# Second stage of a two-stage attention and mixture-of-experts block: bias rows as a matrix product, row sums from the residual addition, squared differences on ScalarE, fewer router steps, a new VectorE order

## The reference

```python
h = layernorm(x) * (1 + ca) + sa
x = x + ga * linear_attention(h)          # ends in out @ w_proj.T + b_proj
h = layernorm(x) * (1 + cb) + sb
x = x + gb * ffn(h)
# ffn: router_input = h * rsqrt(mean(h*h) + 1e-6) * 512**-0.5 * router_scale
#      logits = router_input @ router_logits            (8 experts)
#      probs = softmax(logits); two largest are chosen
#      weights = probs / sum(probs of the chosen two)
#      out = sum over the two of weight * per_expert_scale * expert(h)
```

## Time and profile before

| | |
|---|---|
| median of 3 runs | 2304.57 us (2302.24 to 2309.63) |
| the profiled execution | 2285.14 us, its span 2283.4 us |
| busy: PE, DVE, ACT, POOL | 91%, 62%, 33%, 39% of the span |
| second stage, about | 613 us to 1086 us after the span's start |
| DVE, PE, POOL busy from 699.6 to 1031.6 us | 299.6, 268.7, 252.0 us of 332 |
| granted TensorE clock there | 0.89 |

### The profile page before, as it was taken

One profiled execution on the slowest core, in us unless ns is written; L12 is line 12 of the kernel. 1 busy time (PEld: TensorE's weight loads), 2 busy tenths in 40 slices (PEclk: granted clock), 3 DMA queues, 4 the chain that ended last, 5 costly groups with the idle time before them and its releaser, 6 DMA issues.

```text
span 2283.4 us, 42310 instructions
## 1 busy us (share of the span) xinstructions
PE 2088.3 (91%) x9344; PEld 1632.4 (71%) x9345; DVE 1420.9 (62%) x3309; ACT 757.3 (33%) x1363; POOL 890.2 (39%) x689
## 2 busy tenths in 40 slices
PE   7999999999987888874899999999999989999997
PEld 5688878888655555553678887887778768778886
DVE  6555655565379999895366665665556556556664
ACT  4244434344334344432133332332223223223332
POOL 4475656667427777775011111111111111111111
PEclk9999999999988899986899999999999999999998
DMA  7576555565625566557755557557675775765554
GB/s 244 190 245 206 170 198 162 199 210 189 216 74 187 201 221 227 192 181 289 216 133 129 130 130 222 131 131 195 157 209 130 212 228 131 188 165 128 130 115 79
DMA packets 293177, 404.88 MB, mean 177 GB/s; under 512 B 50510, under 2 KB 188750, under 8 KB 285262
## 3 DMA queue, kind: packets, MB, share of 16 engines
q1 hardware_dynamic: 165104, 257.57, 35.5%
q0 software_dynamic: 30640, 74.29, 15.6%
q10 hardware_dynamic: 97200, 70.82, 9.8%
HBM read 210.57 MB, written 191.98 MB: 176 GB/s over the span
## 4 chain that ended last, share of the span: by engine, by line
PE 42%; DMA 6%; DVE 1%; issue 1%; ACTq 1%; ACT 0%; DVEq 0%; POOL 0%; SPq 0%
PE bank L1774 42%; DMA arow<-act_rows 3%; DMA act_rows<-hact 3%; ACTq L1031 1%; DVE hact L1663 0%; DVE x_t_lo L1657 0%; DVE gbr L1699 0%; DVE act_t_lo L1674 0%; ACT gact L1020 0%; DVEq L1681 0%; DMA meta<-expert_rows 0%; DMA expert_rows<-rows,dest 0%; SPq L551 0%; ACT x_t_hi L1015 0%; DVE orow L1702 0%
## 5 line engine op out<-in xcount | busy, mean ns | idle before, releaser
L1774 PE MATMUL bank<-wbuf,x_t_hi 128*128 x2160 | 679.5, 396 | 46.5 <-DVE x_t_lo L1657 46.1
L782 POOL DMA_INDIRECT out_rows<-orow,cur_tok x135 | 209.0, 1548 | 985.4 <-DVE orow L1702 917.0
L1774 PEld LDWEIGHTS bank<-wbuf,x_t_hi 128*128 128x128 f32 x2160 | 409.4, 190 | 141.1 <-issue 50.7
L1774 PE MATMUL bank<-wbuf,x_t_lo 128*128 x1080 | 424.6, 393 | 0.0
L1774 PE MATMUL bank<-wbuf,act_t_hi 128*128 x1080 | 346.3, 403 | 30.1 <-DVE act_t_lo L1674 29.7
L1663 DVE TENSOR_TENSOR hact<-bank,gact 128x512 f32<-128x512 f32 x135 | 93.2, 691 | 336.9 <-PE bank L1774 301.0
L1774 PEld LDWEIGHTS bank<-wbuf,act_t_hi 128*128 128x128 f32 x1080 | 208.1, 193 | 80.3 <-issue 34.4
L1774 PEld LDWEIGHTS bank<-wbuf,x_t_lo 128*128 128x128 f32 x1080 | 205.3, 190 | 44.5
L1774 PE MATMUL bank<-wbuf,act_t_lo 128*128 x540 | 215.2, 399 | 0.0
L1020 ACT ACTIVATE gact<-bank 128x512 f32<-128x512 f32 x135 | 80.7, 598 | 330.1 <-PE bank L1774 258.1
L745 POOL DMA_INDIRECT expert_rows<-rows,dest x128 | 132.0, 1031 | 102.3 <-DVE dest L1442 67.8
(11 more groups left out here) (218 smaller groups left out, 3993.6 us busy)
## 6 DMA issues: line engine op xcount, KB each, us to landing
wbuf<-expert_split SPq DMA_DIRECT2D x24, 1536.0 KB, 9.1
xrow<-expert_rows SPq DMA_DIRECT2D x540, 64.0 KB, 3.1
act_rows<-hact ACTq DMA_DIRECT2D x135, 256.0 KB
arow<-act_rows ACTq DMA_DIRECT2D x540, 64.0 KB
expert_split<-split_hi SPq DMA_DIRECT2D x32, 768.0 KB, 3.5
expert_split<-split_lo SPq DMA_DIRECT2D x32, 768.0 KB, 5.9
xg<-in_x SPq DMA_DIRECT2D x16, 1024.0 KB, 5.7
q_rows<-qf SPq DMA_DIRECT2D x16, 1024.0 KB, 6.5
```

The source lines that it names most:

```text
L782: pool.indirect_dma_start(out=out, out_offset=bass.IndirectOffsetOnAxis(cur_tok[at][:, 0:1], 0), in_=orow[at % 2][:, :], in_offset=None, c ...
L1774: last = mm(dst, stationary(a, f), moving(b, f), start=(k == 0), stop=(k == parts * n - 1))
```

## The change

Per group of the second stage it removes GpSimd's four `add_bias`. The bias comes into the projection's bank by one more product: `part_r` is a 128 x 128 matrix of 2/128, `bias_r` holds the bias in its high part on the first 64 partitions and the rest on the other 64. `residual` becomes a scalar_tensor_tensor that also writes the row sum; `sums` and `moments` go, `mean` scales two sums at a time, and ScalarE makes (sum - 512 x) squared and its row sum (`off_squared`), from which variance and seed follow. The router drops the softmax's own sum and reciprocal (they cancel in weights / sum of weights), the guard, and two type casts. `recip` moves from the end of the turn before to just behind the first `residual`; `logits` and `largest` move behind all four `divide`; the row numbers (`all_places`) move behind the last `normed`. On ScalarE the order changes too, among it `logits_out`, which now stands behind `square` of tiles 0 and 1.

```diff
@@ gpsimd
-        def add_bias(g, par):
-            pool.wait_ge(s_x2, 16 * (g + 1))
-            for t in range(TPG):
-                pool.tensor_tensor(xb[par][:, t, :], xb[par][:, t, :], gab[:, batch_of(g), :], ALU.add).then_inc(s_xb, 1)
@@ scalar
+        def off_squared(g, t):
+            act.wait_ge(s_x1, TPG * g + t + 1)
+            at_least(act, s_off, TPG * g + t)
+            act.activation(off_out[:, :], x1[:, t, :], ACT.Square, scale=-float(C), bias=sum2[:, t:t + 1],
+                           accum_out=off2[:, t:t + 1]).then_inc(s_off, 1)
@@ scalar group2, the new order
+            rms_seed(g - 1); off_squared(g, 0); h2t_copy(g - 1, 0); h2t_copy(g - 1, 1)
+            off_squared(g, 1); seed2(g, 0); on_hi(g + 1, 1 - par, 0); on_hi(g + 1, 1 - par, 1)
+            h2t_copy(g - 1, 2); h2t_copy(g - 1, 3); off_squared(g, 2); square(g, 0, par); square(g, 1, par)
+            logits_out(g - 1); on_hi(g + 1, 1 - par, 2); on_hi(g + 1, 1 - par, 3); exps(g - 1)
+            off_squared(g, 3); seed2(g, 1); den_out(g + 2); square(g, 2, par); square(g, 3, par)
@@ scalar and vector, once
+        act.activation(part_r[:, :], ones_f[:, :], ACT.Copy, scale=2.0 / P).then_inc(s_bias, 1)
+        act.activation(bias_r[:, :, :], gab[:, :, :], ACT.Copy).then_inc(s_bias, 1)
+        tt(bias_r[P // 2:, :, :], gab[P // 2:, :, :], f32(bias_r[P // 2:, :, :]), ALU.subtract).then_inc(s_bias, 1)
@@ vector
-            tt(x1[:, t, :], Y_B[t % 2][:, :], xb[par][:, t, :], ALU.add).then_inc(s_x1, 1)
+            stt(x1[:, t, :], Y_B[t % 2][:, :], 1.0, xb[par][:, t, :], ALU.mult, ALU.add, accum_out=sum2[:, t:t + 1]).then_inc(s_x1, 1)
-            turn.did(dve.bn_stats(st2[:, t, :], x1[:, t, :]), f"sums{t}")
-            turn.did(dve.bn_aggr(mv2[:, t, :], st2[:, t, :]), f"moments{t}")
+            turn.did(ts(mean2[:, h], sum2[:, h], 1.0 / C, None, ALU.mult), f"mean{half}")
-            ts(ve2[:, h], mv2[:, h, 1], LN_EPS, None, ALU.add).then_inc(s_var2, 1)
+            turn.did(ts(ve2[:, h], off2[:, h], float(C) ** -3, LN_EPS, ALU.mult, ALU.add), f"var{half}")
-            chosen_two, exp_sum, exp_sum_recip, probs, renorm_guard, two_places
-            dve.tensor_copy(dest[par][:, :, :], destf[:, :, :]).then_inc(s_dest, 1)
+                dve.tensor_reduce(dest[par][:, :, :], chosen[:, :, :, :], AX.X, ALU.add).then_inc(s_dest, 1)
@@ vector group2, the new order of a steady turn
+            rms_var(g - 1); residual(g, 0); rms_seed_squared(g - 1); recip(g + 1); rms_seed_error(); residual(g, 1)
+            mean(g, 0); rms(); divide(g + 1, 0); divide(g + 1, 1); var2(g, 0); centred(g, 0); seed_squared(g, 0)
+            centred(g, 1); seed_error(0); residual(g, 2); rstd2_of(0); normed(g, 0); normed(g, 1)
+            divide(g + 1, 2); divide(g + 1, 3); choice(g - 1)        # logits to mask
+            residual(g, 3); mean(g, 1); centred(g, 2); exp_chosen(g - 1); centred(g, 3); renorm(); var2(g, 1)
+            scaled(); seed_squared(g, 1); renorm_recip(); seed_error(1); weights(1 - par); rstd2_of(1)
+            normed(g, 2); normed(g, 3); all_places(g - 1)            # places to destinations
@@ tensor
         def project(g, par, t):
+            at_least(pe, s_x1, TPG * g + t - 1)
+            mm(dst, part_r[:, :], bias_r[:, b, :], start=True, stop=False)
             if t == 0:
                 pe.wait_ge(s_onlo, HG * (g + 1))
-            at_least(pe, s_x1, TPG * g + t - 1)
-            product(Y_B[t % 2][:, :], 3, FC, ...)
+            product(dst, 3, FC, ..., first=False).then_inc(s_y, 1)
```

More of the change, by code:

```diff
@@ L749, in group2 @@
             if has(g, 1):
[L750 to L757, removed]
+                for j in range(HG):
+                    low_on(g + 1, 1 - par, j)
             if g:
@@ L984, in group2 @@
                 den_out(g + 2)
-            if not has(g, 1):
+            if not more:
                 h2t_copy(g, 0)
@@ L1323, in centred @@
             if t % 2 == 0:
-                turn.after(f"moments{t + 1}")
-            turn.did(stt(lnt[t % 2][:, :], x1[:, t, :], mv2[:, t, 0:1], mod_row_of(g, 2), ALU.subtract, ALU.mult), f"centred{t}")
+                turn.after(f"mean{t // 2}")
+            turn.did(stt(lnt[t % 2][:, :], x1[:, t, :], mean2[:, t:t + 1], mod_row_of(g, 2), ALU.subtract, ALU.mult), f"centred{t}")
         def normed(g, t, par):
@@ L1434, in places_chosen, with destinations, all_places, choice @@
             turn.did(tt(chosen[:, :, :, :], pos[:, :, :].unsqueeze(1).to_broadcast([P, 2, TPG, E]), oh[:, :, :, :], ALU.mult), "chosen")
-        def two_places():
+        def destinations(par):
             turn.after("chosen")
-            turn.did(dve.tensor_reduce(destf[:, :, :], chosen[:, :, :, :], AX.X, ALU.add), "two_places")
-        def destinations(par):
-            turn.after("two_places")
-            dve.tensor_copy(dest[par][:, :, :], destf[:, :, :]).then_inc(s_dest, 1)
+            with nc.allow_low_precision("row numbers under 2 ** 24, whole in both types"):
+                dve.tensor_reduce(dest[par][:, :, :], chosen[:, :, :, :], AX.X, ALU.add).then_inc(s_dest, 1)
+        def all_places(g, par):
+            places(g)
+            next_places()
+            places_chosen()
+            destinations(par)
+        def choice(g):
+            logits(g)
+            largest()
+            less_max()
+            where_largest()
+            one_hot()
+            mask()
         def group2(g, par):
-            router = g > 0
-            last = not has(g, 1)
+            router, last = g > 0, not has(g, 1)
             turn.begin(g, ROUTE_STEPS if router else 0)
@@ L1453, in group2 @@
                 rms_seed_squared(g - 1)
-            sums(g, 0)
+            if not last:
+                recip(g + 1)
             if router:
@@ L1457, in group2 @@
             residual(g, 1, par)
-            moments(0)
-            sums(g, 1)
+            mean(g, 0)
             if g == 1:
@@ L1477, in group2 @@
             rstd2_of(0)
-            sums(g, 2)
             normed(g, 0, par)
-            moments(2)
             normed(g, 1, par)
-            if router:
-                logits(g - 1)
             if not last:
                 divide(g + 1, 1 - par, 2)
-            if router:
-                largest()
-            if not last:
                 divide(g + 1, 1 - par, 3)
             if router:
-                less_max()
-                where_largest()
-                chosen_two()
-                one_hot()
-                mask()
+                choice(g - 1)
             residual(g, 3, par)
@@ L1584, in _ @@
         rms()
[L1585 to L1600 removed]
+        choice(NG - 1)
+        all_weights(NG - 1, 1)
+        all_places(NG - 1, 1)
         turn.end(NORM_STEPS)
@@ L1773, in product @@
                 for a, b in PASSES[:parts]:
-                    last = mm(dst, stationary(a, f), moving(b, f), start=(k == 0), stop=(k == parts * n - 1))
+                    last = mm(dst, stationary(a, f), moving(b, f), start=(first and k == 0), stop=(k == parts * n - 1))
                     k += 1
```

188 lines of the change are left out of this document (72 added, 116 removed).

## The result

The changed kernel takes 2332.32 us (median of 10 runs, 2324.96 to 2342.0) where the kernel before takes 2305.99 us in the same comparison (10 runs): a ratio of 1.0116, 95% interval 1.0093 to 1.014. It is slower by 26 us. The forecast was 2263 us, with 2293 as the upper end.

A forecast was written before the change was run, and what follows sets the result against it. The loop through GpSimd (row numbers, scatters, `low_on`, `divide` 3) was taken to bind some turns, TensorE's projections the others. Period 25.56 to 22.7 saves 37 us over 13 turns, first turns 5, tail 0: 2304.6 - 42 = 2263 us, range 2240 to 2293.

The forecast's parts named there:

- `divide` 3 starts at D + 13.7: On VectorE, `divide` 3 waits for GpSimd's eight scatters and two `low_on`, which follow the row numbers.
- The mask is ready at D + 16.7 (16.8): VectorE's router steps behind `divide` 3 end at D + 16.0, plus 0.7 to 0.9 us of blocking by `low_on`.
- `turn_logits` starts at D + 11.8: On TensorE, it waits for `logits_out` behind `square` 1: start at D + 12.6 after some 2.6 us idle.
- New row numbers at D + 23.0 (22.0 or 23.6): Turn period: 22.0 us at full clock, 23.6 where the clock falls and projection 3 is 1.8 us late.
- the price taken: VectorE's row sum in `residual` was taken to cost 0.15 us as an accumulator read.
- the doubled pass: Upper bound for `residual` with its row sum on VectorE: 0.69 us more if the pass doubled.
- The first D: First two turns, with no scatter ahead of `low_on` and much blocking by `add_bias`: 5 us saved.
- The wait for the mask: TensorE's long wait, 4.07 us, was to go, since the mask would be ready before `rank`.
- Near D + 7.9: End of projection 2 on TensorE, from which `residual` 2, `normed` 1 and `logits_out` were timed.
- `divide` 3 not waiting for GpSimd: Sign that the prediction is wrong: it held that `divide` 3 stands behind GpSimd's queue until D + 13.7.
- The slower one: Rival: `logits_out` behind `square` 1, clock already down when `turn_logits` starts; period 26.5 us, 2313 us; chance 0.05.
- 22.7 between 22.0 and 23.6: Mean period taken, some turns at full clock and some with a fallen clock, against 25.56 us before.

The follow-up runs named there:

- c3: The changed kernel unaltered, run again on a chip where signals were on time: 0.9902 of the kernel before, period 23.57 us.
- set 4: Load of `qb` moved behind `residual` 2 in three kernels, beside c3; on the changed kernel the move gave 0.9905 against 0.9902.
- c1: The changed kernel unaltered, measured a second time, with late signals: 0.9938 of the kernel before.
- c2: The changed kernel unaltered, measured a third time, beside the kernel before, with late signals: 0.9961 of the kernel before.
- e1: The changed kernel with `logits_out` ahead of the squares of tiles 0 and 1 on ScalarE: better than c3 by 0.8%.

## Why the prediction was wrong

*What was right.* Let D be the end of the row numbers, as before; in c3 it is 811.89. Projection 2 ends at D + 7.9, as forecast. `divide` 3 starts at D + 13.7, as forecast, after 1.91 and 0.56 us behind GpSimd. The mask is ready at D + 16.7 (16.8). `turn_logits` starts at D + 11.8 after 1.84 us of idle time (12.6 after 2.6). The clock then falls, and projection 3 ends at D + 17.5 (16.5, or 1.8 us later with a fallen clock). New row numbers at D + 23.0 (22.0 or 23.6). `normed` is at 751 ns in c3 (0.75), `one_hot` at 633 (300 to 800), `residual` itself stays at 691 with an accumulator read of 83 ns behind it, 0.07 below the price taken, and the doubled pass didn't come. The first D came 4.4 us sooner (692.63 against 697.00), forecast 5. The wait for the mask is gone.

*The step that failed.* "Near D + 7.9" was read as the end of projection 2, and `residual` 2 was let start there. In the compared run it starts at D + 10.4. The prediction has no term for the time between a product's end and its signal, since in its profile that time was 0.01 us in every turn. It also named `divide` 3 not waiting for GpSimd as a sign of being wrong, and in the compared run `divide` waits 0.9 us in all. The period is 28.25 instead of 22.7: 13 x 5.55 = 72 us. Of the 5.55 us, 4.68 came with the late signals, by the distance to c3's 23.57 on another chip, 61 us in all. The other 0.87 are there without them. The start (D0 3.4 us later instead of 5 sooner: 8 us) and what follows the thirteenth turn (1268.0 us against 1254.0, forecast 0: 14 us) make up the rest of the 94 us between the forecast for the profiled execution (2285.14 - 42 = 2243) and the measured 2337. Of the 14 us, 5 lie in the last two turns (36.5 us against 31.2). The rest is in the third stage, which is the same in both kernels and varies by more than 10 us between the profiles.

*Which rival was it?* The slower one, by its mechanism: `logits_out` behind `square` 1, the clock down before `turn_logits` starts (1.88 us, forecast 1.9), projection 3's end past D + 20.8 (D + 22.6). It was given 0.05, since in the trace before the clock fell after, not with, the end of an idle stretch. In the compared run the stretch is 5.9 us instead of the 2.6 forecast, and in twelve of the thirteen turns the clock fell 1.3 to 4.4 us before it ended. The period it was priced at, 26.5, was 1.75 us short: it had no late `residual`, and no `low_on` on top of `normed` 0 and 1 (3.23 us for the two instead of 1.65).

*A warning that was at hand.* The profiled execution took 2285.14 us and the three timed ones 2302 to 2310. The prediction noted the 19 us and took the difference of one from the median of the other. The sets show what it most likely stood for: before has 2289 to 2291 where the signals are on time and 2306 where they are late, as in the timed ones. None of those three was profiled. For the first kind the forecast is a ratio of 2243 / 2285 = 0.982, measured 0.990: 18 us are missing, and 11 of them (13 x 0.87) are the period, 23.57 and not 22.7. The term that was mis-sized is the share of turns with a fallen clock: 22.7 between 22.0 and 23.6 stands for fewer than half, and in c3 the clock falls behind this idle stretch, or at its end, in 11 of 13 turns. c3's profiled execution (2272.35) is 29 us over 2243: the same 11, 1 at the first row numbers, and 17 behind the thirteenth turn (1271.5 us against 1254.0), of which 14 lie behind the last row numbers. For the second kind the prediction lacked the term that mattered.

*Where the gain went.* Where signals are late, the product alone gives 2.2%, with the short router 2.4%. The remaining parts (row sums, squared differences on ScalarE, the new orders) take about 1.0% of it back where the signals are on time (0.9902 against 0.9807 and 0.9793, other chips) and 2.0% where they are late (0.9961 against 0.9757, one chip). `logits_out` behind the squares accounts for most of this: moved, it returns 0.7 to 1.2%.

*What stays open.* What holds the signal. Late signals of projection 2 were seen only while GpSimd's scatters were being issued or had yet to land: turns 0 and 1, which have none, are always on time. Of 112 late signals of projection 2 in nine profiles, 75 lie within 0.1 us of a landing record of a scatter; a moment taken at random in the 3.6 us behind the product's end would be so near to one in about 35% of the cases. In these profiles some signal records are missing too (51 to 63 of 64 projections have one), in the others none. That ties the delay to the traffic of the scatters on some chips, but doesn't show how. Whether less traffic would shorten it wasn't seen, since set 4 had no delay. Nor is it known why it was 2.4 us in each turn of the first comparison and 0.8 to 3.5 in c1 and c2.

## What to carry to other kernels

Take the distance between a product's last row and the start of its reader as a quantity of its own, and look for it under "remote". If the profiled execution is not in the range of the timed ones, the profile may show another regime than the one that will be compared: price the change for a delay at each hand-over too, by asking what each microsecond there would set off. An engine that waits for a copy should not have that copy queued behind work of a later step: with `logits_out` behind two squares a turn grew by 2.0 to 2.4 us for each microsecond of delay, through TensorE's idle time and clock. With it first the kernel was faster on both chips where the two orders were timed side by side, by 20 and 24 us, though late signals still cost it about 26. And try the parts alone: here one of them was the whole gain.

## What the runs showed of the hardware

- TensorE's signal to other engines came 0.4 to 3.6 us after the end of projection 2 as the profile draws it (2.96 us after the logits product in the turn shown), on some chips and for every kernel there, while GpSimd's indirect transfers were under way. The Trainium skill ("Perfetto Trace Analysis", Tensor Engine Instruction (MATMUL, LD_WEIGHTS)) says that a matmul's drawn end is an estimate and that the semaphore update follows only once the writes are acknowledged. The traces agree in kind: the distance from drawn end to update went from 0.01 us in c3 to 3.45 in c1. That the writes were what came late no run shows.
- The clock: in the turn of c3 shown, after 1.84 us of idle time (from 821.87 to 823.71), the granted clock fell 2.3 us later, at 826.0, for 3.4 us, to 0.50, the level of 1.2 GHz. Idle time of 1.76 us at that place was followed by such a fall in some turns of c3 and not in two. In e1, with less than 0.1 us there, the clock stayed at 1.00 from 816 to 890 us, but it fell at other places of other turns.
- A reduction that writes unsigned integers straight from floats (`dest`, 128x8 from 128x64) takes 220 ns, 10 more than the one in the kernel before that wrote floats (210), so the cast behind it could be dropped at almost no cost.
